# A masked depthwise convolution with divisive normalisation: a zero column in the image rows, PSUM places by slot, and the pooling sums spread over four units

## What is computed

```python
pooled = x.mean(axis=(2, 3))
t = relu(gamma * (pooled @ w1.T - running_mean) * rsqrt(running_var + EPS) + beta)
wt = (t @ w2.T + b2).reshape(b * 96, 1, 3, 3) * MASK      # up-left, up, up-right, left
out = conv(x, wt, padding=1, groups=b * 96) + bias
denom_sq = einsum('nchw,ic->nihw', out * out, gamma_eff) + beta_eff
result = out * rsqrt(denom_sq)
```

## Time and profile before

| what | us |
|---|---|
| median of 3 runs (216.86 to 218.19) | 217.0 |
| time of the profiled execution | 217.67 |
| its span, first to last instruction | 215.9 |
| DVE busy | 187.5 |
| ACT busy | 163.1 |
| PE busy | 160.8 |
| POOL busy | 151.5 |
| mean granted TensorE clock | 0.995 |

### The profile page before, as it was taken

The page is one execution under the profiler, slowest core; times in us unless marked ns, Lnnn a source line. Parts: engine busy times, 40 slices in busy tenths (PEclk is TensorE's granted clock), DMA queues, the critical chain, the costliest instruction groups (busy, mean ns, idle before and its releaser), DMA issues.

```text
span 215.9 us, 2839 instructions
## 1 busy us (share of the span) xinstructions
PE 160.8 (74%) x962; PEld 61.2 (28%) x962; DVE 187.5 (87%) x224; ACT 163.1 (76%) x179; POOL 151.5 (70%) x80
## 2 busy tenths in 40 slices
PE   0018300298899988898999898989998979799960
PEld 0014300132335232323362323233623232323220
DVE  3896199959999999999999999999999999999590
ACT  2336556937994999999949998999494949399880
POOL 2000033244899699999996999999969888889910
PEclk9999999999999999999999999999999999999997
DMA  6999928903978999989999999855554737377596
GB/s 212 421 412 408 386 57 289 320 29 69 298 270 303 374 297 357 376 294 319 321 343 365 309 331 373 297 216 163 203 219 149 242 122 243 125 242 248 164 357 207
DMA packets 16532, 57.89 MB, mean 268 GB/s; under 512 B 2371, under 2 KB 2374, under 8 KB 16518
## 3 DMA queue, kind: packets, MB, share of 16 engines
q1 hardware_dynamic: 14208, 51.52, 65.3%
q10 hardware_dynamic: 2310, 6.19, 10.8%
HBM read 26.24 MB, written 25.17 MB: 238 GB/s over the span
## 4 chain that ended last, share of the span: by engine, by line
DVE 44%; POOL 17%; PE 15%; DMA 6%; ACT 5%; issue 5%; SPq 2%; ACTq 1%; DVEq 0%; POOLq 0%
DVE acc L496 26%; DVE y L496 15%; POOL work L536 11%; PE acc L453 10%; DMA ximg<-in_x 6%; POOL work L530 6%; SPq L259 2%; DVE work L521 2%; ACT work L370 2%; PE acc L451 2%; PE den L470 2%; ACT acc L362 2%; ACTq L379 1%; DVE y L515 1%; PE den L434 1%
## 5 line engine op out<-in xcount | busy, mean ns | idle before, releaser
L496 DVE SCALAR_TENSOR_TENSOR acc<-ximg,taps,acc 128x1016 f32<-128x1016 f32 x82 | 104.7, 1277 | 12.8 <-ACT acc L362 5.9
L536 POOL TENSOR_TENSOR work<-y,work 128x1024 f32<-128x1024 f32 x45 | 106.2, 2377 | 11.0 <-ACT work L395 10.9
L470 PE MATMUL den<-work,gam_e 96*32 96x512 f32 x540 | 80.7, 594 | 1.6 <-ACT taps L349 1.1
L471 PE MATMUL den<-sqd,gam_e 96*32 96x512 f32 x180 | 80.4, 594 | 0.0
L530 POOL TENSOR_TENSOR work<-y 128x1024 f32<-128x1024 f32 x24 | 45.4, 1893 | 42.4 <-DVE y L515 42.3
L496 DVE SCALAR_TENSOR_TENSOR y<-ximg,taps,acc 128x1016 f32<-128x1016 f32 x48 | 61.1, 1273 | 1.7
L453 PE MATMUL acc<-ximg,diag 128*128 128x512 f32 (+1 forms) x112 | 54.4, 608 | 0.0
L395 ACT ACTIVATE work<-den,beta_e 128x1024 f32<-128x1024 f32 x45 | 49.7, 1104 | 4.9 <-PE den L471 4.9
L327 ACT ACTIVATE pool_out<-ximg 128x1920 bf16<-128x1920 f32 (+2 forms) x22 | 41.0, 1865 | 10.1 <-DMA ximg<-in_x 9.2
L362 ACT ACTIVATE acc<-ximg,par_s,taps 128x1024 f32<-128x1024 f32 x34 | 40.7, 1199 | 3.9 <-DVE y L515 3.9
L470 PEld LDWEIGHTS den<-work,gam_e 96*32 96x32 f32 x540 | 21.3, 109 | 55.4 <-issue 52.5
(11 more groups left out here) (52 smaller groups left out, 50.4 us busy)
## 6 DMA issues: line engine op xcount, KB each, us to landing
out_y<-work SPq DMA_DIRECT2D x45, 512.0 KB, 3.6
ximg<-in_x SPq DMA_DIRECT2D x36, 512.0 KB, 6.9
ximg<-in_x SPq DMA_DIRECT2D x12, 576.0 KB, 7.8
sqd<-work ACTq DMA_DIRECT2D x45, 128.0 KB, 3.4
out_y<-work SPq DMA_DIRECT2D x2, 384.0 KB, 4.9
out_y<-work SPq DMA_DIRECT2D x4, 192.0 KB, 3.7
sqd<-y SPq DMA_DIRECT2D x3, 128.0 KB, 3.0
par_s<-in_par ACTq DMA_DIRECT2D x1, 281.0 KB, 4.6
```

The costliest lines, as they stand in the source:

```text
L470: nc.tensor.matmul(den[own, n % 2, j:j + BANK], gam_e[:, own], held(n)[0:C, j:j + BANK], start=True, stop=True)
L471: ins = nc.tensor.matmul(den[C:P, n % 2, j:j + BANK], gam_e[:, s * CD:(s + 1) * CD], sqd[:, t % 2, j:j + BANK], start=True, stop=True)
L496: return nc.vector.scalar_tensor_tensor(out=tap_to(dst, tap), in0=tap_in(n, tap), scalar=tap_w(b, s, tap), in1=tap_to(src, tap), op0=ALU.m ...
L536: nc.gpsimd.tensor_tensor(held(n), result(n), held(n), ALU.mult).then_inc(scaled, 1)
```

## The change

- **Zero column.** Rows in SBUF and in the input array have 129 columns (`WP`), the first of them zero, so a tap that reaches past an edge reads the zero there (for up-right the zero of the next row). Each add covers 8 by 128 elements, the copy is gone, and `convolved` counts once per block instead of twice. An image load is 129/128 as long.
- **PSUM by slot.** One tensor `psum` of four places. Block n's base goes to place n mod 3. `den` of slot 1 shares place 1 with the bases of slot 1; `den` of slots 0 and 2 share place 3. So bases of slots 0 and 2 wait for `convolved` of n-3, a base of slot 1 for the root of block n-6 (which `den` left in that place), `den` of slot 1 for `convolved` of block n+3, `den` of slot 2 for the root of slot 0 of its own unit, `den` of slot 0 for the root of slot 2 of the unit before. The sums for the weights use the second banks of places 2 and 3.
- **Sums.** The six pieces are summed 1, 2, 2, 1 in units 0, 1, 2, 3. POOL squares slot 1 only in units 1 and 2 of the first three images, ACT in units 0 and 3. In unit 3 the order on ACT is root, sum, hidden values, square.
- **Start.** The last piece is summed in three parts; the hidden value is made in two steps by DVE; slot 0's weights come by a product of their own; ACT and DVE each write half of block 0's base. Slot 2 of unit 0 gets its base from PE. PE runs six idle products more at two places (after the first weights, and before the base of unit 1).

```diff
+SUMMED_IN = ((0,), (1, 2), (3, 4), (5,))
...
+    WP = W + 1
...
-        acc = ctx.enter_context(nc.psum_tensor("acc", [P, 2, N], F32))
-        den = ctx.enter_context(nc.psum_tensor("den", [P, 2, N], F32))
+        psum = ctx.enter_context(nc.psum_tensor("psum", [P, SLOTS + 1, N], F32))
...
         def sums_pools(t):
-            return t % UNITS < TAPS_UNIT and t // UNITS < B - 1
+            return len(SUMMED_IN[t % UNITS]) > 1 and t // UNITS < B - 1
...
         def sums(n):
-            return acc[:, n % 2]
+            return psum[:, n % SLOTS]
+
+        def den(n):
+            k = {LAST - 2: 0, LAST: 0, LAST + 1: 1, LAST + 2: SLOTS, FOURTH: 2}.get(n, 1 if n % SLOTS == 1 else SLOTS)
+            return psum[:, k]
+
+        def wait_den_place(pe, n):
+            if n == LAST - 2:
+                pe.wait_ge(convolved, LAST + 1)
...
+            elif n % SLOTS == 1 and n < LAST:
+                pe.wait_ge(convolved, n + SLOTS + 1)
+            elif n == LAST or n % SLOTS == 2:
+                pe.wait_ge(normed, n - 1)
+            elif n > 0:
+                pe.wait_ge(normed, n)
...
         def pool_next(act, t, k):
             b, u = divmod(t, UNITS)
-            if b < B - 1 and u < TAPS_UNIT:
-                i = 2 * u + k
-                pool_on_act(act, b + 1, i, "all", ACT_POOLS + b * len(PIECES) + 2 * u + (1 - k))
+            if b < B - 1 and k < len(SUMMED_IN[u]):
+                i = SUMMED_IN[u][k]
+                pool_on_act(act, b + 1, i, "all", i, ACT_POOLS + b * len(PIECES) + i)
...
+        def wait_sums_place(engine, n):
+            if n % SLOTS == 1 and n >= 2 * SLOTS:
+                engine.wait_ge(normed, n - 2 * SLOTS + 1)
+            elif n >= SLOTS:
+                engine.wait_ge(convolved, n - SLOTS + 1)
...
+        def hidden_sums(pe, b, t):
+            pe.wait_ge(pooled_act, pools_done(b))
+            wait_sums_place(pe, at(t, 2))
+            for i, (_, s) in enumerate(PIECES):
+                ins = hidden_sum(hid_in(t), s, part[:, i:i + 1], i == 0, i == LAST_PIECE)
...
             for j in range(N // BANK):
+                if j > 0 and u == TAPS_UNIT and b < B - 1:
+                    pe.wait_ge(hid_normed, b + 2)
...
             add_tap(n, last, sums(n), result(n)).then_inc(convolved, 1)
-            edge = slice(W - 1, W) if last == UP_RIGHT else slice(0, 1)
-            nc.vector.tensor_copy(in_rows(result(n))[:, :, edge], in_rows(sums(n))[:, :, edge]).then_inc(convolved, 1)
...
                 rsqrt(act, at(t - 2, 2))
-                pool_next(act, t, 1)
+                pool_next(act, t, 0)
                 if chain:
-                    hidden(act, b + 1, hid_place(t))
+                    hidden(act, b + 1, t)
                 square(act, at(t, 1))
-                pool_next(act, t, 0)
+                pool_next(act, t, 1)
...
             first_hidden_sums(pe)
-            tap_sums(pe, 0, 1)
+            first_tap_sums(pe)
+            keep_awake(SLOTS)
...
+                if t == 1:
+                    pe.wait_ge(convolved, SLOTS)
+                    keep_awake(SLOTS)
                 base_on_pe(pe, at(t, 2))
...
+            for i, part_of, col in POOL_ON_DVE:
+                if part_of == "mid":
+                    begin_first_hidden(dve)
+                pool_on_dve(dve, i, part_of, col)
+            first_hidden(dve)
+            first_base(dve)
```

More of the change, by code:

```diff
@@ L352, in diagonals, with first_base_on_act @@
+        def first_base_on_act(act):
+            act.wait_ge(first_tap_ready, 1)
+            nc.scalar.activation(in_rows(sums(0)[:, 0:HALF]), tap_in(0, UP)[:, 0:UR // 2], ACT.Identity,
+                                 bias=bias_s[:, 0:1], scale=tap_w(0, 0, UP)).then_inc(based_act, 1)
         def diagonals(act, b):
@@ L394, in rsqrt @@
             s = n % SLOTS
-            nc.scalar.activation(held(n), den[:, n % 2], ACT.Abs_reciprocal_sqrt, bias=beta_e[:, s:s + 1]).then_inc(normed, 1)
+            nc.scalar.activation(held(n), den(n), ACT.Abs_reciprocal_sqrt, bias=beta_e[:, s:s + 1]).then_inc(normed, 1)
         def rsqrt_last(act, k):
@@ L399, in rsqrt_last, with hidden_sum @@
             act.wait_ge(summed, LAST + k + 1)
-            nc.scalar.activation(held(n)[0:C, lo:hi], last_den(n)[:, lo:hi], ACT.Abs_reciprocal_sqrt,
+            nc.scalar.activation(held(n)[0:C, lo:hi], den(n)[0:C, lo:hi], ACT.Abs_reciprocal_sqrt,
                                  bias=beta_e[0:C, 0:1]).then_inc(normed, 1)
-        def hidden_sum(n, s, col, first, last):
-            return nc.tensor.matmul(hid_in(n), w1r[:, s].rearrange("p t g -> p (t g)"), col, start=first, stop=last)
-        def keep_awake(n):
+        def hidden_sum(to, s, col, first, last):
+            return nc.tensor.matmul(to, w1r[:, s].rearrange("p t g -> p (t g)"), col, start=first, stop=last)
@@ L410, in keep_awake @@
+        def keep_awake(k):
             for _ in range(WAKING):
-                nc.tensor.matmul(den[:, n % 2, 0:BANK], bias_p[:, 0], ones[:, :], start=True, stop=True)
+                nc.tensor.matmul(psum[:, k, 0:BANK], bias_p[:, 0], ones[:, :], start=True, stop=True)
         def first_hidden_sums(pe):
-            end = len(PIECES)
-            order = ((0, pooled_act, 1), (2, pooled_act, 2), (1, pooled_dve, 1), (4, pooled_act, 3),
-                     (3, pooled_dve, 2), (LAST_PIECE, pooled_act, 4), (end, pooled_dve, 3))
@@ new lines, in first_hidden_sums, with first_tap_sums @@
+            s = PIECES[LAST_PIECE][1]
+            pe.wait_ge(pooled_act, ACT_POOLS)
+            hidden_sum(last_hid_in(), s, part[:, 6:7], True, False)
+            pe.wait_ge(pooled_dve, len(POOL_ON_DVE))
+            hidden_sum(last_hid_in(), s, part[:, 7:8], False, True).then_inc(hid_summed, 1)
+        def first_tap_sums(pe):
+            pe.wait_ge(hid_ready, 1)
+            nc.tensor.matmul(first_taps_in(), w2_s[:, 0], hid[:, :], start=True, stop=True).then_inc(first_tap_summed, 1)
+            for s in range(1, SLOTS):
+                ins = nc.tensor.matmul(taps_in(0)[:, s * TAPS:(s + 1) * TAPS], w2_s[:, s], hid[:, :], start=True, stop=True)
+            ins.then_inc(taps_summed, 1)
@@ L749 @@
     }
-    rows = np.pad(np.asarray(x), ((0, 0), (0, 0), (1, 0), (0, 0)))
+    rows = np.pad(np.asarray(x), ((0, 0), (0, 0), (1, 0), (1, 0)))
     B, _, H, W = x.shape
```

223 lines of the change are left out of this document (127 added, 96 removed).

## The result

The changed kernel takes 235.7 us (median of 4 runs, 233.75 to 238.98), the kernel before 216.9 (median of 4 runs): 1.081 times as long, 95% interval 1.076 to 1.087. Ratios and intervals leave out the runs that took over 1.5% more than the fastest of the same kernel; medians are of all runs. The forecast was 220.7, with a range of 216.5 to 229.5. The sign was right, the size was not: 18.8 us more instead of 3.7. The profiled execution took 233.75 us, its span is 231.8 with a mean granted clock of 0.932.

What follows compares the result with a forecast made beforehand. The prediction found four engines within 5% and followed DVE's adds and waits: convolution 164.5 + 18.0 = 182.5 instead of 176.9, start -1.9, so 217.67 becomes 221.4, as a median 220.7 us; range 216.5 to 229.5.

Steps and rivals of the forecast that it cites:

- the 4.8 forecast: Unit 3, slot 2: DVE waits 4.8 us for PE's base, queued behind products needing the sixth pooling sum; before, 0.32.
- the block pitch of 3.84: DVE's time for a block with three adds, once the copy is gone: 3.84 us; with two adds, 2.52.
- rival B: Unit 3: PE's idle 4.3 us lowers its clock, 3.7 us more per image change, 223 to 232 us; chance 0.34.
- The three image changes: DVE's stalls from the sixth pooling sum in unit 3: 5.6 us the first, 6.1 each other, 17.8 for three.
- ACT's lag in the first image: ACT's square in unit 3 starts 0.4 us after DVE ends slot 2 of unit 2, against 0.9 us otherwise.
- the steps behind the base: From DVE's start of slot 2 in unit 3 to the next unit's second block: 7.2 us with the new root wait.
- the 0.2 for unit 0: DVE waits in unit 0 from ACT falling behind: 0.1 us twice, raising 17.8 to 18.0.
- the start: Work from the last piece's landing at 20.0 to block 0: ready at 24.1 instead of 26.06, gain 1.9 us.
- the end: From DVE's last add on: the same chain of move, square, product, root and multiplication stands, so 0 change.
- the three gains: No copy, PSUM by slot and the start: about 14 us together, given back by the sixth pooling sum.
- the late sum: The sixth pooling sum, issued by ACT in unit 3, holds PE's products and base: 18.0 us, bounds 15 to 19.
- the copy: DVE's copy of 0.16 us behind each block's last add: dropping it saves 0.08 us, 1.19 instead of 1.27.

## Why the prediction was wrong

**Right: the mechanism and its timing.** The products with the partial sums wait for a sum issued in the same unit, and PE's base waits behind them. In the second image change each step up to the products came within 0.05 us, and at the full clock DVE's wait is 4.57 us for the 4.8 forecast. That no other wait for PE would be left, and the block pitch of 3.84, hold as well.

**The failed step: the clock (rival B, 0.34).** I took no fall because an idle time of 4.3 us is nearer to 1.5 than to 17, so the sum runs the small products and the base behind them at the upper level. The clock fell three times out of three. From the start of the products to DVE's add the sum has 1.53 + 4.06 = 5.6 us; measured were 8.8, 9.6 and 8.1, which makes 3.2, 4.0 and 2.5 us, 9.7 in all, where rival B had put 3.7 each. The three image changes cost 9.1, 9.9 and 8.4 us instead of 5.6, 6.1 and 6.1: 27.4 for 17.8. ACT's lag in the first image, 0.9 us and not 0.4, adds 0.5 to this, and the steps behind the base took 0.3 less than forecast. The kernel with PE kept busy gets back 11 us by the ratios. The distance between two far rows was no ground for a choice; the rule that rival B took from the Trainium skill, "TensorE: Matmul & The Clock Gate", pointed the right way, and I should have given it the larger chance. The range held only a part of a third fall.

**What is left.** Rival B as priced ends at 232 us, so three falls alone do not reach 235.7. The profiled execution is 12.4 us above its forecast of 221.4: 9.6 for the image changes, 1.0 for small waits of DVE elsewhere (1.2 instead of the 0.2 for unit 0, in single waits of up to 0.17 us, in units 1 to 3), 0.9 at the start, 0.7 at the end, 0.2 outside the span. The median lies another 2 us above it.

**Missed: falls elsewhere.** `den` waits for roots now (6.9 us in eight waits; the kernel before has no such wait in its units), and the idle products of unit 1 wait for DVE, so the clock can drop at other places too. In unit 1 it did in the profiled execution, after 2.98 us without work:

```profile
35.38 1.74 PE L465 MATMUL psum<-ones,bias_p 96*128 96x512 bf16 x6 [2.98 <-DVE y L586]
```

DVE had no wait there. At the end a fall cost 3.2 us in the kernel with the sums back. The changed kernel's runs lie between 233.75 and 238.98 us, with mean clocks of 0.932 down to 0.916; the two longest have the lowest clocks. The profiled one was the shortest. More falls in the others would explain why the median lies 2 us above it, but only the profiled one can be read.

**Mis-sized: the start.** 1.0 us instead of 1.9. DVE's third of the last piece ended at 22.0 instead of 21.5, because DVE first waited 0.93 us for PE's earlier products; the products and small steps behind it took another 0.4 us more than I took them, and block 0 started at 25.04.

**Mis-sized: the three gains.** The prediction puts them at 14 us, so without the late sum the forecast would be 220.7 - 18.0 = 202.7. The kernels with the sums back take 213.8 and, with a busy end, 210.5. The prediction dropped all 8.1 us of DVE's waits; in the latter kernel 6.5 us are still there (167.2 us from block 0's start to the last block's, where blocks of 3.84 and 2.52 us make 160.7), 1.6 of them at each image change. So part of what the prediction booked on the late sum is there without it. The late sum costs 22 us on either kernel, and the gains are 4 us, or 7 with a busy end.

**Mis-sized: the copy.** Its 0.08 us per block are there in the timeline, but ACT is so near to DVE's pace that only 0.9 of 3.8 us show in the time once all else is in order.

**The end.** From DVE's last add at 218.2 on, the end took 13.6 us, 0.7 more than before; what of that is PE and what DVE's slower multiplications (1308 ns against 1095 before) was not separated.

## What to carry to other kernels

A step that is moved later within a period must be followed through the queue of whoever waits for it: here 2 us of ACT work left PE idle for 4.2 us each time and made DVE wait 4.6 us even at the full clock, because PE's base stood behind the wait. If such a wait leaves PE without work for a few microseconds, count with the lower clock behind it, and price what runs there at half rate; a busy filler held the clock in two of three image changes. And when four engines are within 5% of each other, a gain on one of them mostly turns into waits for the next: of 3.3 us of copy time taken from DVE, 0.9 showed.

## What the runs showed of the hardware that was not expected

- The granted clock fell in six image changes out of six in which PE had been idle for 3.9 to 4.2 us (three in the changed kernel, three with the late sum alone).
- After shorter idle times the outcome varies. Of the seven kernels with the new start, six show a fall in unit 1 after 2.8 to 3.4 us without work and one, after 2.7 us, none. At the end, after the same 2.21 us, two of four profiled executions show a fall and two, the changed kernel's among them, none.
- Twelve products of one column, each behind a load of 128 columns of weights, take 1.5 us in which PE counts as busy in the profile, but they did not hold the clock: with 4 us of dense products ahead of them it still fell once in three, and in the kernel with the base ahead of them it was at 0.50 behind them in all three image changes. What of that is the products and what the short waits around them (0.2 to 0.8 us) was not separated.
- A stretch at the lower clock lasts: in the changed kernel's image changes the clock was back at 1.00 only some 5.5, 6 and 3 us after PE had begun its base, which is most of the price.
- The granted clock of the windows does not show every such stretch: in the kernel before it reads 1.00 where the bias product takes 0.59 us. The lengths of the products are the surer sign.
